# Gating products inside the layernorm ahead of the routing, and mixture weights built as a row on the chip: a two-block graph network with feed-forward stages

## The chip, the cores and the metric

One Trainium2 chip, one core. The time is that of the device for one execution of the whole kernel, in microseconds (us), as the median of three runs.

## What is computed

The reference takes a graph of 3125 nodes with 256 features and 103125 edges, and adds four residual stages to the node features, each on a layernorm of them. Two of the four matter here:

```python
# stage 2: experts; x is the layernorm of the node features
logits = einsum('bsd,de->bse', x, gate_w) + gate_b      # 16 experts
probs = softmax(logits)
top_probs, top_idx = top_k(probs, 2)
...
# stage 4: a mixture of depths over the nodes; x is again a layernorm
weights = (einsum('bsd,do->bso', x, wr) + br)[..., 0]    # one number a node
_, idx = top_k(weights, 1562); sel_idx = idx[:, :1561]
h = gelu(x[sel_idx] @ w1 + b1);  y = h @ w2 + b2         # hidden width 1024
y = y * weights[sel_idx]
processed = zeros_like(x).at[sel_idx].set(y);  out = processed + x
```

Stages 1 and 3 are graph attention networks with 8 heads and with three layers; the change leaves them alone.

## The kernel before

Everything is float32 in what follows. The nodes are 25 blocks of 128 (`NB`), the last with 53 rows. The program is a row of phases. A phase is a function under `@phase`: it allocates its semaphores, writes one instruction stream an engine, and at its end `run` clears its semaphores and puts a barrier of all engines. So nothing of a phase starts before everything of the phase ahead of it has ended, and a transfer that the phase's SyncE stream waits for holds up that end.

**From the first layernorm sum to the experts.** `node_phase` with the name n1 loads the input `x` and the attention output `y` in five parts of five blocks, adds them, takes the statistics, and normalizes block by block on VectorE (line 597). TensorE transposes each block's two halves (line 644) into one of four PSUM buffers, ScalarE copies them to `xt` (line 629). SyncE stores the sum to `x1` (two transfers, `store_nodes`) and the normalized rows to `xn1` (five transfers, line 544), and waits for all seven at the end (line 547). Then `router_phase` starts: it loads the gate's weights and bias, and TensorE multiplies each block of `xt` with the two halves of the gate's weights into one PSUM bank (lines 1466 to 1471):

```python
pe.wait_ge(s_in, 32)
for b in range(NB):
    for k in range(2):
        last = nc.tensor.matmul(ps[:, b * XE:(b + 1) * XE], xt[:, k, b * P:(b + 1) * P], gw[:, k, :],
                                start=k == 0, stop=k == 1)
last.then_inc(s_l, 1)
```

VectorE waits for the last of these (`s_l`), adds the bias (line 1508), and goes through softmax, top two, ranks and slots, a chain on VectorE with a few products between. `moe_phase` gathers rows of `xn1` by the slots.

**The mixture phase.** `node_phase` with the name n3 makes the last `xt` and `xn`, and `mod_phase` follows. Its SyncE stream loads wr, br, w1, b1, w2, b2 in this order, then the residual rows `res`. TensorE makes the weights as 50 products with one moving column (line 1842), one PSUM column a block, and then runs to the end without VectorE: hidden products of 320 columns for five blocks at a time (line 1855), and between them the output products of the five blocks before (line 1866). ScalarE applies the gelu (line 1886) and copies outputs to `ff` (line 1892). VectorE adds br to the weights (line 1906). SyncE stores them to `w_dram` (line 1814), waits, and loads them back broadcast to all partitions as a row of 3200 (line 1816). Against that row VectorE counts for each node how many weights are larger (lines 1913 to 1925), finds the nodes among the first 1561, and then, as `ff` comes, multiplies and adds into `res` (lines 1937, 1939), which SyncE stores in parts. GpSimd adds `xn` into `res` (line 1835) once `res` has landed.

What sets the order is each engine's own stream as written, and one in-order queue of transfers on SyncE. A float32 product is two weight loads and two matmul instructions in the trace, so 50 products are 100; a transpose is one of each. A name such as `xt1` or `n1_x` stands in the trace without its number.

## Time and profile before

| | |
|---|---|
| median of 3 runs | 4057.14 us (4055.54 to 4057.16) |
| the profiled execution's own time | 4054.18 us |
| its span | 4052.5 us |
| busy share of the span | PE 86%, PEld 64%, DVE 71%, ACT 59%, POOL 5% |
| mean granted TensorE clock | 0.947 |
| n1, from its first load's issue to the routing phase's first | 2042.92 to 2090.38 us |
| routing phase, to the experts' first load | 2090.38 to 2175.26 us |
| mixture phase, to the span's end | 3845.07 to 4052.5 us |

All times inside the trace count from the span's start. PE is TensorE's matmul, PEld its weight load, DVE VectorE, ACT ScalarE, POOL GpSimd, SP SyncE; a q behind a name is that engine's sequencer. A PEclk of 1.00 is the full clock, 2.4 GHz, and 0.50 the lower, 1.2 GHz. The duration of a merged row runs from the first instruction's start to the last one's end. Matmuls are pipelined: one lasts longer than the distance to the next.

### The profile page before, as it was taken

Reading aid. Unit: us, or ns where it says so; the run is one execution under the profiler, and the core shown is the slowest. Engines: PE = TensorE matmul, PEld = TensorE weight load, DVE = VectorE, ACT = ScalarE, POOL = GpSimd, SP = SyncE. Lnnn points to the kernel's source line nnn. Section 1 sums busy time; section 2 is a strip of 40 time slices with the busy share of each in tenths; the row PEclk is TensorE's granted clock in tenths of the full one; section 3 lists DMA queues with packets and bytes.
Section 4 is the critical chain, followed back from the end, with each engine's and each line's share of the span. In section 5 each row is a group of like instructions: output and inputs, shape, how many; then the busy total and the mean of one; then the engine's idle time right before and its main releaser. Section 6 shows DMA issues by size and latency. Waiting matters only on the chain. (4 is left out here: it accounts for less than half of the span.)

```text
span 4052.5 us, 69131 instructions
## 1 busy us (share of the span) xinstructions
PE 3497.2 (86%) x26175; PEld 2605.0 (64%) x26176; DVE 2880.4 (71%) x4370; ACT 2400.7 (59%) x3733; POOL 218.0 (5%) x212
## 2 busy tenths in 40 slices
PE   4989738888888888888835999689998999899799
PEld 2545436666666666666633566478887888788687
DVE  6989849999999999999934222365646654655456
ACT  3777628888888888888810111256665665444422
POOL 0000000000000000000001444100000000000010
PEclk9999969999999999999957999799999999999889
DMA  1222331111114111111145422233223232333220
GB/s 50 98 88 98 117 101 50 68 60 58 67 51 183 63 68 51 67 56 63 36 132 178 128 44 45 59 131 112 96 96 112 96 112 80 127 112 112 87 63 32
DMA packets 135864, 349.43 MB, mean 86 GB/s; under 512 B 28251, under 2 KB 106462, under 8 KB 117886
## 3 DMA queue, kind: packets, MB, share of 16 engines
q1 hardware_dynamic: 114840, 320.24, 22.3%
q0 software_dynamic: 13888, 20.07, 2.7%
q10 hardware_dynamic: 6822, 4.85, 0.4%
q8 instruction: 207, 3.39, 0.3%
q14 instruction: 107, 0.88, 0.1%
HBM read 279.91 MB, written 65.20 MB: 85 GB/s over the span
## 5 line engine op out<-in xcount | busy, mean ns | idle before, releaser
L919 PE MATMUL hd_psT<-ident,hd_scores 128*128 128x128 f32 (+1 forms) x5000 | 738.2, 286 | 31.8 <-ACT hd_scores L822 31.8
L831 ACT ACTIVATE hd_probsT<-hd_psT 128x768 f32<-128x768 f32 (+1 forms) x800 | 648.2, 835 | 187.3 <-PE hd_psT L919 186.4
L867 DVE SCALAR_TENSOR_TENSOR hd_scores<-hd_el,hx 128x3136 f32<-128x3136 f32 x200 | 695.5, 3478 | 24.4 <-DMA hd_mask<-mask_dram 18.4
L871 DVE CUSTOM_DVE_ANT_0 hd_scores<-hd_scores,hd_mask 128x3136 f32<-128x3136 f32 x200 | 684.0, 3420 | 8.6
L933 PE MATMUL hd_psO<-hd_probsT,hx 128*32 128x128 f32 (+1 forms) x10000 | 583.3, 286 | 101.0 <-ACT hd_probsT L831 100.2
L919 PEld LDWEIGHTS hd_psT<-ident,hd_scores 128*128 128x128 f32 (+1 forms) x5000 | 544.3, 143 | 185.5 <-issue 183.6
L822 ACT ACTIVATE hd_scores<-hd_scores,hd_negmax 128x1664 f32<-128x1664 f32 (+1 forms) x400 | 640.7, 1602 | 11.0 <-DVE hd_negmax L871 10.9
L1309 PE MATMUL ly_psO<-hx_a,ly_probsT 128*128 128x256 f32 x2500 | 583.1, 381 | 0.0
L1267 ACT ACTIVATE ly_probsT<-ly_psT 128x768 f32<-128x768 f32 (+1 forms) x300 | 249.3, 831 | 469.5 <-PE ly_psT L1298 469.4
L933 PEld LDWEIGHTS hd_psO<-hd_probsT,hx 128*32 128x32 f32 (+1 forms) x10000 | 322.8, 110 | 300.0 <-ACT hd_probsT L831 176.2
L1309 PEld LDWEIGHTS ly_psO<-hx_a,ly_probsT 128*128 128x128 f32 x2500 | 453.3, 189 | 71.2 <-issue 16.6
L366 PE MATMUL cnt<-onehot_c,onehot_dst_a 128*128 128x392 bf16 x1200 | 237.8, 335 | 89.9 <-DVE onehot_c L308 81.8
L308 DVE TENSOR_SCALAR onehot_c<-iotaC,stage_c 128x392 bf16<-128x392 f16 x1200 | 294.1, 314 | 0.0
L1309 PE MATMUL ly_psO<-hx_b,ly_probsT 128*128 128x256 f32 x1250 | 291.7, 381 | 0.0
L1298 PE MATMUL ly_psT<-ident,ly_scores 128*128 128x128 f32 x1875 | 258.9, 276 | 35.1 <-ACT ly_scores L1258 35.1
L366 PEld LDWEIGHTS cnt<-onehot_c,onehot_dst_a 128*128 128x128 bf16 x1200 | 135.1, 128 | 208.9 <-issue 113.0
L1258 ACT ACTIVATE ly_scores<-ly_scores,ly_negmax 128x1664 f32<-128x1664 f32 (+1 forms) x150 | 239.6, 1598 | 39.0 <-DVE ly_negmax L1179 38.5
L1298 PEld LDWEIGHTS ly_psT<-ident,ly_scores 128*128 128x128 f32 x1875 | 219.6, 141 | 62.7 <-ACT ly_scores L1258 35.8
L1179 DVE CUSTOM_DVE_ANT_0 ly_scores<-ly_scores,ly_mask 128x3136 f32<-128x3136 f32 x75 | 256.5, 3420 | 3.2
L1673 PE MATMUL moe_ps_h<-moe_w,moe_xT 128*128 x512 | 243.4, 598 | 8.6 <-SPq L1631 7.3
L1309 PEld LDWEIGHTS ly_psO<-hx_b,ly_probsT 128*128 128x128 f32 x1250 | 226.7, 189 | 35.5 <-issue 8.3
L1731 ACT ACTIVATE moe_hidden<-moe_ps_h 128x512 f32<-128x512 f32 x64 | 38.2, 597 | 326.6 <-PE moe_ps_h L1673 326.6
(298 smaller groups left out, 3805.2 us busy)
## 6 DMA issues: line engine op xcount, KB each, us to landing
ly_mask<-mask_dram SPq DMA_DIRECT2D x75, 1568.0 KB, 6.5
hd_mask<-mask_dram SPq DMA_DIRECT2D x50, 1568.0 KB, 6.8
mask_dram<-logc SPq DMA_DIRECT2D x200, 196.0 KB, 1.9
moe_w<-in_L_ffn_w SPq DMA_DIRECT2D x48, 512.0 KB, 10.9
hd_el<-el_dram SPq DMA_DIRECT2D x5, 1568.0 KB, 9.9
hd_el<-el_slope_dram SPq DMA_DIRECT2D x4, 1568.0 KB, 12.9
x<-n_x SPq DMA_DIRECT2D x2, 3072.0 KB
n_x<-in_x SPq DMA_DIRECT2D x8, 640.0 KB, 7.7
```

The lines of the kernel that those rows point to most:

```text
L308: last = nc.vector.tensor_scalar(oc[:, k, :], g["iotaC"][:, :], c[:, k:k + 1], None, ALU.is_equal)
L366: last = nc.tensor.matmul(o, ohA[:, s, :, k], ohC[:, s, k, :], start=k == 0 and not further, stop=True, skip_group_check=True)
L822: nc.scalar.activation(sc[:, u % 3, halves[j]], sc[:, u % 3, halves[j]], ACT.Exp, scale=-1.0, bias=nm[:, u % 3:u % 3 + 1], accum_out=den[: ...
L831: nc.scalar.activation(pT[:, gi % 2, 0:w], psT[gi % 2][:, 0:w], ACT.Copy).then_inc(s_ev, 1)
L867: nc.vector.scalar_tensor_tensor(sc[:, c, :], el[:, h, 0, :], hx[:, b, o:o + 1], el[:, h, 1, :], ALU.subtract, ALU.min).then_inc(s_lk, 1)
L871: nc.vector.tensor_tensor_reduce(out=sc[:, c, :], in0=sc[:, c, :], in1=mask[:, B % 2, :], scale=1.0, scalar=3.0e38, op0=ALU.add, op1=ALU.m ...
L919: last = nc.tensor.transpose(psT[gi % 2][0:r, t * P:(t + 1) * P], sc[:, u % 3, c0:c0 + r], g["ident"][:, :])
L933: last = nc.tensor.matmul(psO[B % 3][cg * CH:(cg + 1) * CH, h * P:(h + 1) * P], hx[0:r, tt, c0:c0 + CH], pT[0:r, gi % 2, t * P:(t + 1) * P ...
L1179: nc.vector.tensor_tensor_reduce(out=sc[:, c, :], in0=sc[:, c, :], in1=mask[:, B % 2, :], scale=1.0, scalar=3.0e38, op0=ALU.add, op1=ALU.m ...
L1267: nc.scalar.activation(pT[:, gi % 2, 0:w], psT[gi % 2][:, 0:w], ACT.Copy).then_inc(s_ev, 1)
L1298: last = nc.tensor.transpose(psT[gi % 2][0:r, t * P:(t + 1) * P], sc[:, B % 3, c0:c0 + r], g["ident"][:, :])
L1309: last = nc.tensor.matmul(psO[B % 2][:, 0:D], pT[0:r, gi % 2, t * P:(t + 1) * P], hx[B // NB % 2][0:r, tt, 0:D], start=tt == 0, stop=tt == ...
```

## The change

Two parts.

**Routing.** A new phase, `routed_nodes_phase`, holds n1 and the routing. It owns the tiles `x` and `xn`, the PSUM bank of the logits, and a semaphore `s_stored` that outlives n1. Inside n1 TensorE makes the gating products of block b-2 behind the transposes of block b, each waiting for ScalarE's copy of that block; the gate's weights are loaded behind n1's other loads. n1's SyncE no longer waits for its seven stores; the routing's SyncE does, at its end. The routing starts with the bias load alone, and VectorE waits for that in place of `s_l`. Since the new phase wraps two, one more clearing of semaphores and one more barrier stand behind the routing.

**Mixture weights.** TensorE makes the row itself: wr, one half at a time, broadcast to all 128 columns as the stationary operand, against `xt` as the moving one, in eight chunks of 400 columns over two PSUM banks (16 products, 32 matmul instructions). ScalarE adds br on its way to the row. VectorE gets each block's weights down the partitions by multiplying the block's piece of the row with the identity and summing. The store and the load of `w_dram` go. br is now awaited with wr, ahead of TensorE's first product.

```diff
 def node_phase(...):
+        if s_kept is not None:
+            s_out = s_kept
@@ sync
+                if gate is not None:
+                    sp.dma_start(gw[:, :, :], gate_dram.rearrange("(k p) n -> p k n", p=P)).then_inc(s_gw, 16)
...
-                if x_out is not None:
+                if x_out is not None and s_kept is None:
                     sp.wait_ge(s_out, 32 + (16 * NPART if xn_store is not None else 0))
@@ tensor
+            def gating(b):
+                pe.wait_ge(s_xt, b + 1)
+                for k in range(2):
+                    nc.tensor.matmul(logits[:, b * XE:(b + 1) * XE], xt[:, k, b * P:(b + 1) * P], gw[:, k, :],
+                                     start=k == 0, stop=k == 1)
+            if gate is not None:
+                pe.wait_ge(s_gw, 16)
             for b in range(NB):
...
                 last.then_inc(s_T, 1)
+                if gate is not None and b >= 2:
+                    gating(b - 2)
+            if gate is not None:
+                gating(NB - 2)
+                gating(NB - 1)
 def router_phase(...):
@@ sync
-            sp.dma_start(gw[:, :, :], a["L0_ffn_gate_w"].rearrange("(k p) n -> p k n", p=P)).then_inc(s_in, 16)
...
+            sp.wait_ge(s_kept, n_kept)
             sp.wait_ge(s_clear, 16 * len(spare))
@@ tensor
-            pe.wait_ge(s_in, 32)
-            for b in range(NB):
-                for k in range(2):
-                    last = nc.tensor.matmul(ps[:, b * XE:(b + 1) * XE], xt[:, k, b * P:(b + 1) * P], gw[:, k, :],
-                                            start=k == 0, stop=k == 1)
-            last.then_inc(s_l, 1)
@@ vector
-            dve.wait_ge(s_l, 1)
-            dve.wait_ge(s_in, 32)
+            dve.wait_ge(s_in, 16)
+@phase
+def routed_nodes_phase(nc, g, x_in, y_dram, x1, xn1, tok, wgt, tile_e, a):
+    with ExitStack() as ctx:
...
+        s_stored = new_semaphore(nc, g, "rn_s_stored")
...
+            node_phase(nc, g, "n1", xt, x_in=x_in, y=y, y_in=y_dram, x_out=x1, xn_out=xn, xn_store=xn1, x_tile=x,
+                       gate=(a["L0_ffn_gate_w"], gw, logits), s_kept=s_stored)
+        router_phase(nc, g, logits, s_stored, 32 + 16 * NPART, tok, wgt, tile_e, (x1, xn1), a)
 def mod_phase(...):
@@ sync
-            sp.dma_start(br[:, :], line(a["L1_ffn_br"], 1)).then_inc(s_in, 16)
+            sp.dma_start(br[:, :], line(a["L1_ffn_br"], 1)).then_inc(s_wr, 16)
...
-            sp.wait_ge(s_wt, 1)
-            sp.dma_start(g["w_dram"].rearrange("(b p) -> p b", p=P), wt[:, :], allow_slow_non_contiguous=True).then_inc(s_wd, 16)
-            sp.wait_ge(s_wd, 16)
-            sp.dma_start(row[:, :], line(g["w_dram"], NP)).then_inc(s_row, 16)
@@ tensor
-            pe.wait_ge(s_wr, 16)
-            for b in range(NB):
+            pe.wait_ge(s_wr, 32)
+            for c in range(WCHUNKS):
+                if c >= 2:
+                    pe.wait_ge(s_row, c - 1)
                 for k in range(2):
-                    last = nc.tensor.matmul(psw[:, b:b + 1], xt[:, k, b * P:(b + 1) * P], wr[:, k:k + 1],
-                                            start=k == 0, stop=k == 1)
-            last.then_inc(s_w, 1)
-            pe.wait_ge(s_in, 80)
+                    last = nc.tensor.matmul(psw[c % 2][:, 0:WCOLS], wr[:, k:k + 1].broadcast_to([P, P]),
+                                            xt[:, k, c * WCOLS:(c + 1) * WCOLS], start=k == 0, stop=k == 1)
+                last.then_inc(s_w, 1)
+            pe.wait_ge(s_in, 64)
@@ scalar
-            act.wait_ge(s_in, 80)
+            act.wait_ge(s_wr, 32)
+            for c in range(WCHUNKS):
+                act.wait_ge(s_w, c + 1)
+                nc.scalar.activation(row[:, c * WCOLS:(c + 1) * WCOLS], psw[c % 2][:, 0:WCOLS], ACT.Identity,
+                                     bias=br[:, :]).then_inc(s_row, 1)
+            act.wait_ge(s_in, 64)
@@ vector
-            dve.wait_ge(s_w, 1)
-            dve.wait_ge(s_in, 80)
-            nc.vector.tensor_scalar(wt[:, :], psw[:, 0:NB], br[:, :], None, ALU.add).then_inc(s_wt, 1)
             c.wait()
-            dve.wait_ge(s_wt, 1)
-            dve.wait_ge(s_row, 16)
+            for b in range(NB):
+                dve.wait_ge(s_row, ((b + 1) * P - 1) // WCOLS + 1)
+                nc.vector.scalar_tensor_tensor(spread[:, b, :], row[:, b * P:(b + 1) * P], 1.0, g["ident"][:, :],
+                                               ALU.mult, ALU.mult, accum_out=wt[:, b:b + 1]).then_inc(s_wt, 1)
+            dve.wait_ge(s_wt, NB)
+            dve.wait_ge(s_row, WCHUNKS)
             dve.wait_ge(s_k, 5)
+            dve.wait_ge(s_in, 64)
```

How the instructions stand on TensorE at the first place, n1 to the routing, before (a product counts once here; `n_ps` holds transposes, `rt_ps` the logits):

```order
L634 UNCONDITIONAL_BRANCH
L644 MATMUL n_ps<-ident,n_xn 128x128 x50
L492 UNCONDITIONAL_BRANCH
L1464 UNCONDITIONAL_BRANCH
L1469 MATMUL rt_ps<-rt_gate_w,xt 128x16 x50
L1476 MATMUL rt_ps_within<-rt_one_hot,rt_before 128x384
```

And with the change, the beginning and the end of that stretch (`rn_ps_logits` is the logits' bank):

```order
L641 UNCONDITIONAL_BRANCH
L658 MATMUL n_ps<-ident,rn_xn 128x128 x6
L646 MATMUL rn_ps_logits<-gate_w,xt 128x16 x2
L658 MATMUL n_ps<-ident,rn_xn 128x128 x2
...
L658 MATMUL n_ps<-ident,rn_xn 128x128 x2
L646 MATMUL rn_ps_logits<-gate_w,xt 128x16 x6
L492 UNCONDITIONAL_BRANCH
L1481 UNCONDITIONAL_BRANCH
L1487 MATMUL rt_ps_within<-rt_one_hot,rt_before 128x384
```

Six transposes stand ahead of the first products, then two and two take turns, and the last three blocks' products end the phase; the routing has none left.

On ScalarE at the second place, n3 to the mixture phase, with the change (line 636 copies n3's transposes, 1908 makes the row, 1919 is the gelu):

```order
L636 ACTIVATE xt<-n_ps 128x2x128 x25
L492 UNCONDITIONAL_BRANCH
L1903 UNCONDITIONAL_BRANCH
L1908 ACTIVATE mod_weights_row<-mod_psw,mod_br 128x400 x8
L1919 ACT_TABLE_LOAD
L1919 ACTIVATE mod_hidden<-mod_h,mod_b 128x320 x32
```

The eight passes of the row stand where there was nothing before; the table load ahead of the gelu stays where it was, and none is added.

## Rows read from the trace of the kernel before

**Rows 1.** the chain that ended last, in time order: start us, us, what
```profile
3845.07 2.02 DMA mod_wr<-in_L_ffn_wr
...
3847.14 21.49 PE mod_w L1842 x100
3868.63 37.52 PE mod_h L1855 x128
```

**Rows 2.** timeline, layernorm to routing: start us, us, engine, what [idle before <-releaser]
```profile
2072.91 8.19 PE L644 MATMUL n_ps<-ident,n_xn 128*128 128x128 f32 x50 [37.59 <-DVE n_xn L597]
2073.64 7.88 ACT L629 ACTIVATE xt<-n_ps 128x256 f32<-128x256 f32 x25 [1.57 <-PE n_ps L644]
2074.18 8.95 SPq L544 DMA_DIRECT2D xn_dram<-n_xn  x5
2090.38 0.38 SPq L1434 DMA_DIRECT2D rt_gate_w<-in_L_ffn_gate_w  x1
...
2094.08 21.52 PE L1469 MATMUL rt_ps<-rt_gate_w,xt 128*128 128x16 f32 x100 [12.97 <-DMA rt_gate_b<-in_L_ffn_gate_b]
...
2115.63 0.57 DVE L1508 TENSOR_TENSOR rt_logits<-rt_ps,rt_gate_b 128x400 f32<-128x400 f32 x1 [24.72 <-PE rt_ps L1469]
```

**Rows 3.** DMA issue of that stretch: count, KB, us from issue to landing
```profile
rt_gate_b<-in_L_ffn_gate_b SPq DMA_DIRECT2D x1, 8.0 KB, 3.2
```

**Rows 4.** stretches: us, busy PE, PEld, DVE, ACT, POOL, PEclk, DMA, GB/s
```profile
2074.90:2075.90 1.00, 1.00 (x7) 1.00 (x7) 1.00 (x4) 0.90 (x3) 0.00 (x0) 0.62 1.04 348
...
2094.00:2115.00 21.00, 20.92 (x98) 20.92 (x99) 0.00 (x0) 0.00 (x0) 0.21 (x1) 0.50 0.11 9
```

**Rows 5.** timeline of TensorE's weight loads in the second network's projection
```profile
2627.46 0.40 PEld L1114 LDWEIGHTS np_e<-ident,hx_a 128*128 128x128 f32 x2
2627.78 0.25 PEld L1099 LDWEIGHTS np_x<-ident,np_xn 128*128 128x128 f32 x2
2628.00 0.74 PEld L1107 LDWEIGHTS np_h<-wx,np_xT 128*128 128x128 f32 x4
2628.77 0.41 PEld L1114 LDWEIGHTS np_e<-ident,hx_a 128*128 128x128 f32 x2
```

**Rows 6.** the gating products' instructions: ns min/median/max
```profile
L1469 PEld LDWEIGHTS rt_ps<-rt_gate_w,xt x100: 288/333/337, 2094.1 to 2115.2; 128*128 128x128 f32 x100
L1469 PE MATMUL rt_ps<-rt_gate_w,xt x100: 374/374/396, 2094.1 to 2115.2; 128*128 128x16 f32 x100
```

**Rows 7.** timeline, last layernorm to the mixture phase
```profile
3835.53 8.75 ACT L629 ACTIVATE xt<-n_ps 128x256 f32<-128x256 f32 x25 [1.57 <-PE n_ps L644]
...
3845.49 0.46 SPq L1806 DMA_DIRECT2D mod_br<-in_L_ffn_br  x1
...
3867.80 13.70 POOL L1835 TENSOR_TENSOR mod_res<-mod_res,xn 128x6400 f32<-128x6400 f32 x1 [21.72 <-DMA mod_res<-x]
...
3868.49 28.78 PE L1855 MATMUL mod_h<-xt,mod_w 128*128 128x320 f32 x95
...
3872.35 0.53 ACT L1886 ACTIVATE mod_hidden<-mod_h,mod_b 128x320 f32<-128x320 f32 x1
...
3891.20 3.34 DVE L1918 TENSOR_SCALAR_CACHE_REDUCE mod_junk<-mod_weights_row,mod_weights 128x2997 bf16<-128x2997 f32 x1 [22.29 <-DMA mod_weights_row<-w_dram]
...
3894.46 0.35 DVE L1921 SCALAR_TENSOR_TENSOR mod_junk<-mod_weights_row,mod_weights,mod_low 128x128 bf16<-128x128 f32 x1
```

**Rows 8.** stretches of that phase, columns as in rows 4
```profile
3847.00:3852.00 5.00, 4.86 (x23) 4.86 (x24) 0.00 (x0) 0.00 (x0) 0.00 (x0) 0.52 0.91 268
3852.00:3857.00 5.00, 5.00 (x25) 5.00 (x25) 0.00 (x0) 0.00 (x0) 0.00 (x0) 0.50 0.95 301
3873.00:3875.00 2.00, 2.00 (x6) 1.29 (x5) 0.00 (x0) 0.56 (x2) 2.00 (x1) 0.63 0.04 0
```

**Rows 9.** timeline: its last hidden block, and VectorE behind the counting
```profile
3992.24 17.39 PE L1855 MATMUL mod_h<-xt,mod_w 128*128 128x320 f32 x64
...
4013.54 0.42 DVE L1937 TENSOR_TENSOR mod_tmp<-hx_b,mod_b 128x256 f32<-128x256 f32 x1 [4.40 <-ACT hx_b L1892]
```

More of the change, by code:

```diff
@@ L485, in node_phase @@
 def node_phase(nc, g, name, xt, x_in=None, y=None, y_in=None, x_out=None, unit=False, xn_out=None, xn_store=None,
-               gelu=False, layernorm=True, add_loops=False):
+               gelu=False, layernorm=True, add_loops=False, x_tile=None, gate=None, s_kept=None):
     with ExitStack() as ctx:
@@ L500, in node_phase @@
         if layernorm:
-            x = sb("x", [P, NB, D])
+            x = x_tile if x_tile is not None else sb("x", [P, NB, D])
             xn = xn_out if xn_out is not None else sb("xn", [P, NB, D])
@@ L512, in node_phase @@
             loop = lambda i: lv[:, i, :].rearrange("p (q o) -> p q o", o=1)
+        if gate is not None:
+            gate_dram, gw, logits = gate
+            s_gw = sem("s_gate_w")
+        if s_kept is not None:
+            s_out = s_kept
         block = ctx.enter_context(nc.Block())
@@ L646, in _ @@
                 last.then_inc(s_T, 1)
+                if gate is not None and b >= 2:
+                    gating(b - 2)
+            if gate is not None:
+                gating(NB - 2)
+                gating(NB - 1)
 @phase
@@ L1421, in router_phase @@
         s_din, s_dout = sem("s_diagonal_in"), sem("s_diagonal_out")
[L1422 removed]
         psw = ctx.enter_context(nc.psum_tensor("rt_ps_within", [P, 512], F32))
         pst = ctx.enter_context(nc.psum_tensor("rt_ps_total", [P, 512], F32))
[L1425 to L1426 removed]
+        s_in, s_io, s_c, s_z, s_e, s_one, s_hot, s_rank, s_zero, s_clear, s_sel, s_inv = (
+            sem(n) for n in ("s_in", "s_io", "s_c", "s_z", "s_e", "s_one", "s_hot", "s_rank", "s_zero", "s_clear",
                              "s_selectors", "s_inverse"))
@@ L1577, in _ @@
             step(nc.vector.tensor_copy(wgt[:, :], back[:, 2, :]))
+@phase
+def routed_nodes_phase(nc, g, x_in, y_dram, x1, xn1, tok, wgt, tile_e, a):
+    with ExitStack() as ctx:
+        tile = lambda n, s: ctx.enter_context(nc.sbuf_tensor(f"rn_{n}", s, F32))
+        s_stored = new_semaphore(nc, g, "rn_s_stored")
+        x = tile("x", [P, NB, D])
+        xn = tile("xn", [P, NB, D])
+        logits = ctx.enter_context(nc.psum_tensor("rn_ps_logits", [P, 512], F32))
+        with ExitStack() as first:
+            xt = first.enter_context(nc.sbuf_tensor("xt1", [P, 2, NP], F32))
+            y = first.enter_context(nc.sbuf_tensor("y1", [P, NB, D], F32))
+            gw = first.enter_context(nc.sbuf_tensor("gate_w", [P, 2, XE], F32))
+            node_phase(nc, g, "n1", xt, x_in=x_in, y=y, y_in=y_dram, x_out=x1, xn_out=xn, xn_store=xn1, x_tile=x,
+                       gate=(a["L0_ffn_gate_w"], gw, logits), s_kept=s_stored)
+        router_phase(nc, g, logits, s_stored, 32 + 16 * NPART, tok, wgt, tile_e, (x1, xn1), a)
 @phase
@@ L1790, in mod_phase @@
         hid = sb("hidden", [P, 2, MB, CT * P])
+        spread = sb("spread", [P, NB, P])
+        WCHUNKS = 8
+        WCOLS = NP // WCHUNKS
         res = sb("res", [P, NB, D])
@@ L1794, in mod_phase @@
         pso = [ctx.enter_context(nc.psum_tensor(f"mod_o{i}", [P, 512], F32)) for i in range(2)]
-        psw = ctx.enter_context(nc.psum_tensor("mod_w", [P, 512], F32))
-        names = ("s_wr", "s_in", "s_k", "s_w", "s_wt", "s_wd", "s_row", "s_res", "s_sum", "s_h", "s_hid", "s_o", "s_ff", "s_c",
+        psw = [ctx.enter_context(nc.psum_tensor(f"mod_psw{i}", [P, 512], F32)) for i in range(2)]
+        names = ("s_wr", "s_in", "s_k", "s_w", "s_wt", "s_row", "s_res", "s_sum", "s_h", "s_hid", "s_o", "s_ff", "s_c",
                  "s_y1", "s_y2", "s_st")
-        (s_wr, s_in, s_k, s_w, s_wt, s_wd, s_row, s_res, s_sum, s_h, s_hid, s_o, s_ff, s_c, s_y1, s_y2, s_st) = (
+        (s_wr, s_in, s_k, s_w, s_wt, s_row, s_res, s_sum, s_h, s_hid, s_o, s_ff, s_c, s_y1, s_y2, s_st) = (
             sem(n) for n in names)
@@ L1979, in program @@
         tile_e = sb("tile_expert", [1, NT], I32)
-        with ExitStack() as s:
-            xt = s.enter_context(nc.sbuf_tensor("xt1", [P, 2, NP], F32))
-            with nc.sbuf_tensor("y1", [P, NB, D], F32) as y:
-                node_phase(nc, g, "n1", xt, x_in=a["x"], y=y, y_in=y_dram, x_out=x1, xn_store=xn1)
-            router_phase(nc, g, xt, tok, wgt, tile_e, (x1, xn1), a)
+        routed_nodes_phase(nc, g, a["x"], y_dram, x1, xn1, tok, wgt, tile_e, a)
         moe_phase(nc, g, tile_e, tok, wgt, xn1, x1, a)
```

7 lines of the change are left out of this document (1 added, 6 removed).

## The prediction, made before the change was run

> **What bounds the kernel now.** I read the chain that ended last first. It is followed back to the start of the mixture phase and is TensorE nearly throughout: 2.02 us for the load of wr, 21.49 us for the mixture weights, then hidden and output products to the end [rows 1]. So in that phase a microsecond saved on TensorE ahead of the hidden products is one off the total, and the work on VectorE is not: late in the phase VectorE sits idle 4.40 us until ScalarE hands it an output [rows 9].
>
> Then I read the timeline from the second layernorm to the routing, which says what ends each wait there. TensorE's transposes end at 2072.91 + 8.19 = 2081.1, ScalarE's copies at 2081.5, and SyncE has issued its last store by 2083.1, but the next phase begins at 2090.38 [rows 2]. The end of n1 thus hangs on the stores. Then TensorE idles 12.97 us in all until the gate's bias has landed, runs 21.52 us, and VectorE starts at 2115.63, released by TensorE [rows 2]. Behind that the routing is a chain on VectorE, so what counts there is the start of line 1508.
>
> Last I read the granted clock in both places. It is 0.50 in the whole stretch of gating products [rows 4], and rises only some way into the hidden products: its mean over 3873 to 3875 is 0.63 [rows 8], so the last 0.5 us of those ran at full clock and it rose at 3874.5, 6.0 us after the hidden products began at 3868.49 [rows 7].
>
> The profiled execution took 4054.18 us, 3.0 less than the median of 4057.14. The sum is made against the former, and 3.0 is added at the end. A measurement of this kernel can tell some 0.2% (8 us) from no change.
>
> **Part one, n1 and the routing.** Removed from the path: the stores' wait, and the gate's weight load ahead of the products. Added to n1's TensorE stream: 100 instructions to 50. At 1.2 GHz one gating instruction comes every 21.52 / 100 = 0.215 us [rows 2]. Each lasts 0.374 us and its load 0.333 [rows 6], so loads overlap products, and with 16 columns moving it is the 128x128 load that sets 0.215. A transpose has a load of the same shape, so I give it 0.215 too. The lower bound is the pace VectorE gave it, 8.19 / 50 = 0.164. With 150 x 0.215 = 32.3 us from 2072.91 the stream ends at 2105.2 (lower bound 2102.6), the last product 0.16 later.
>
> The change of phase then costs what it costs between n3 and the mixture phase, where no store holds it: ScalarE ends at 3835.53 + 8.75 = 3844.28 [rows 7] and the first load goes out at 3845.07 [rows 1], 0.8 us. So the routing begins at 2106.2, and now waits for the bias alone, which takes 3.2 us from its issue [rows 3]. VectorE starts at 2109.4 in place of 2115.6: **6.2 us gained**. The stores were down by 2090 before, so they hide under the longer products and the wait at the routing's end, 60 us on, costs nothing. The weight load behind n1's loads has over 10 us until the first transpose.
>
> What goes the other way is the clearing and barrier behind the routing. No row shows one alone. It costs between nothing and a whole change of phase, 0.8; I take half, **0.4 us lost**.
>
> The clock is my main choice here. In n1 it rose within a stretch of pure transposes: its mean over 2074.9 to 2075.9 is 0.62 [rows 4], so it rose near 2075.7, 2.8 us after they began [rows 2]. For all 21 us of pure gating products it stayed at 0.50 [rows 4]. In the change six transposes come alone, 1.3 us of them, and then four gating instructions to two transposes. I take the mixture for the kind that holds two thirds of it: 1.2 GHz throughout. The Trainium skill, page "TensorE: Matmul & The Clock Gate", section "Part 4: PE-mode transpose", says that transposes don't count as activity that brings the full clock. By that rule the forecast for this part is certain and its rival below impossible. The trace does not agree: only transposes ran when the clock rose in n1 [rows 2, 4].
>
> **Part two, the mixture phase.** TensorE now waits for br as well, issued at 3845.49 [rows 7]. Its landing isn't shown; the gate's bias, broadcast in the same way, took 3.2 us [rows 3], wr's load 2.02 [rows 1]. I take 3.2: TensorE starts at 3848.7, not 3847.14 (1.6 lost; with 2.0 it would be 0.4).
>
> Its 32 instructions have 400 columns. At full clock 64 of 320 columns took 17.39 us, 0.272 each [rows 9], so 400 take 0.340, and twice that at half clock. They are dense from the start, and in the rows at hand such work waits 2.8 to 6.0 us for the clock; I take the middle, 4.4, of which half is lost: 32 x 0.340 + 2.2 = 13.1 us, to 3861.8. With 2.8 and 6.0 it is 0.8 less or more.
>
> Are w1, b1, w2, b2 there by then? They are 2.2 MB, and at 268 and 301 GB/s [rows 8] 1.34 MB had moved by 3852 and the rest by 3855. Yes. So hidden products begin at 3861.8 in place of 3868.49, and at full clock: before, the first 6.0 us at half clock held 11 instructions (6.0 / 0.544), now they take 3.0. The eleventh ends at 3864.8 in place of 3874.5: **9.7 us gained**, and from there TensorE does what it did.
>
> ScalarE's eight passes: one over 320 columns took 0.53 [rows 7], so 400 cost 0.53 to 0.66, against 1.36 us that TensorE needs for a chunk at full clock; two banks cover it. VectorE's 25 products with the identity: one of that size took 0.35 [rows 7], with the read of the sum I take 0.4 each. They follow the chunks; the last four come behind the last chunk, and counting starts near 3864.5 in place of 3891.20 [rows 7]. These 27 us are worth nothing: the 22.29 us wait for the row [rows 7] was never TensorE's. They are also the cover if GpSimd's add of 13.70 us [rows 7], so far beside an idle VectorE, and the counting now slow each other. If that cover went, the end of VectorE's 25 residual blocks would be late next.
>
> **Sum.** 6.2 - 0.4 + 9.7 = 15.5. 4054.2 - 15.5 = 4038.7, and with 3.0 for the median **4041.7 us**. The likeliest case's own range: the pace of transposes (2.6 less), the barrier and br's load (0.4, 1.2), the clock's rise (0.8), and up to 1.6 either way because later phases meet the clock at another moment: 4038 to 4045.
>
> **Rivals.**
> *The clock rises in n1's mixture.* For it: transposes alone raised it [rows 4]. Against it: they are a third of the instructions, and their neighbours left it at 0.50 for 21 us. In the second network's projection, at full clock, eight loads take 1.31 us, four of them under 258 columns [rows 5], which at 0.272 x 258/320 = 0.219 [rows 9] leaves 0.108 for each load-bound one. 13 instructions at 0.215, then 137 at 0.108 make 17.6 us in place of 32.3: 14.7 more gained, **4027 us**.
>
> *Hidden products don't start earlier*, because their weights share the queues with the residual rows' load, which lands at 3867.80 [rows 7]. Then only 0.7 us of part two is left: 4054.2 - 6.2 + 0.4 - 0.7 + 3.0 = **4050.7**. Against it speaks the sum of bytes above.
>
> *Slower: the turns on TensorE in n1.* Each change between transposes and products has a semaphore wait in front. If the load behind it can't go ahead under the instruction before, load and product stand one after the other, 0.333 + 0.374 [rows 6] in place of 0.215: 0.49 us, 50 changes, 24.6 us. 4041.7 + 24.6 = **4066**. It outweighs the gains from 32 such changes on. Against it: in the projection, three kinds take turns with waits between them, and the eight loads show no such gap [rows 5].
>
> That the stores are still waited for in n1 is no rival of weight: by 2105 they are long down.
>
> **Chances.** The forecast 0.80, the clock in the mixture 0.07, hidden products held 0.08, exposed loads 0.03, and 0.02 for gains too small to measure. Faster by over 0.2% are the first two, 0.87; within 0.2% the third and the last, 0.10; slower 0.03. The range 4036 to 4051 holds the likeliest case with its bounds and reaches the second rival; it leaves out the ends at 4027 and 4066.
>
> **What would show it.** In n1: 150 instructions on TensorE in some 32 us at 0.50, the next phase within 1 us of their end, line 1518 (the old 1508) 36.5 us after the first transpose, 42.7 before. In the mixture phase: the first 400-column product 3.6 us after the phase's start, a pace that halves some 4 us on, hidden products at 0.272 from the first on and 16.7 us after the phase's start, 23.4 before. It is wrong if the clock in n1 reads 1.00 behind the first blocks, if the first hidden product waits for a DMA, or if VectorE's residual blocks end the phase without idle time before them.

## The result and the profile after

Medians of six runs each: 4055.41 us before (4053.95 to 4057.16), **4038.91 us after** (4037.66 to 4040.6). The ratio is 0.9958 with a 95% interval of 0.9946 to 0.9969: faster by 0.42%. The profiled execution took 4037.66 us (4054.18 before), its span is 4036.0, the mean granted clock 0.949. Three other executions (one of the kernel before, beside the runs below, one of part two alone, one of the last run) took 1.3 to 2.3 times as long at a granted clock of 0.63 or less, and the medians leave them out.

The chain that ended last in the kernel after, in time order (start us, us, what), to be laid beside [rows 1]:

```profile
3838.28 3.38 DMA mod_br<-in_L_ffn_br
...
3841.70 13.51 PE mod_psw L1870 x32
3855.22 34.45 PE mod_h L1883 x128
```

It starts with br's load now, 3.38 us, in place of wr's. The phase begins at 3837.86, TensorE 3.84 us later, and the hidden products 17.4 us after the phase (23.6 before). The phase lasts 4036.0 - 3837.86 = 198.1 us, where it lasted 4052.5 - 3845.07 = 207.4: **9.3 us** from part two.

Timeline of the kernel after, n1 to the routing (columns as in rows 2), beside [rows 2]:

```profile
2073.09 1.51 PE L658 MATMUL n_ps<-ident,rn_xn 128*128 128x128 f32 x6 [37.88 <-DVE rn_xn L604]
...
2075.10 0.67 PE L658 MATMUL n_ps<-ident,rn_xn 128*128 128x128 f32 x2
...
2076.28 0.67 PE L658 MATMUL n_ps<-ident,rn_xn 128*128 128x128 f32 x2
...
2100.20 2.58 PE L646 MATMUL rn_ps_logits<-gate_w,xt 128*128 128x16 f32 x12
...
2103.58 0.34 SPq L1451 DMA_DIRECT2D rt_gate_b<-in_L_ffn_gate_b  x1
...
2106.10 0.57 DVE L1518 TENSOR_TENSOR rt_logits<-rn_ps_logits,rt_gate_b 128x400 f32<-128x400 f32 x1 [1.98 <-DMA rt_gate_b<-in_L_ffn_gate_b]
```

TensorE's 150 instructions run from 2073.09 to 2102.78, 29.7 us, and a round of two transposes and four products takes 2076.28 - 2075.10 = 1.18 us. The routing begins 0.8 us behind the last product, and VectorE waits 1.98 us for the bias. From the first transpose to its logits are 33.0 us, before 42.7 [rows 2]: 9.7 us. The windows of that stretch (columns as in rows 4) have the clock at 0.50 all along; the last of them:

```profile
2090.00:2100.00 10.00, 10.00 (x53) 10.00 (x53) 0.00 (x0) 3.35 (x9) 0.00 (x0) 0.50 0.00 0
```

At the routing's end, timeline before and then after (VectorE's first and last instruction behind the inverse, then the experts' first load):

```profile
2173.12 0.36 DVE L1574 COPY rt_slot_source<-rt_ps_inverse 128x192 f32<-128x192 f32 x1 [8.37 <-PE rt_ps_inverse L1485]
...
2174.06 0.19 DVE L1577 COPY slot_gate<-rt_slot_source 128x64 f32<-128x64 f32 x1
2175.26 0.93 SPq L1624 DMA_DIRECT2D moe_w<-in_L_ffn_w  x2
```

```profile
2164.73 0.36 DVE L1584 COPY rt_slot_source<-rt_ps_inverse 128x192 f32<-128x192 f32 x1 [9.51 <-PE rt_ps_inverse L1496]
...
2165.67 0.19 DVE L1587 COPY slot_gate<-rt_slot_source 128x64 f32<-128x64 f32 x1
2167.26 0.42 SPq L1651 DMA_DIRECT2D moe_w<-in_L_ffn_w  x1
```

Before, VectorE's last instruction ends at 2174.25 and the load goes out 1.01 us later; now it is 1.40: the additional clearing and barrier cost 0.39 us. The routing's chain itself is 59.8 us long, from 2106.10 to 2165.86, where it was 58.6; VectorE waits 9.51 us for TensorE's inverse in place of 8.37. That is 1.1 us lost that the prediction didn't have, and it is the clock: from the logits' addition to the first of the 100 products of the inverse are 38.7 us in both traces, but the granted clock rose 3.3 us into them before and 5.6 us into them now, and they took 18.7 and 19.8 us. Over all traces on record it rises 2.9 to 6.0 us in, and they take 18.5 to 20.0; the run with GpSimd's add moved, whose routing is the change's, has 2.9 and waits only 8.20 us. So this loss is no added work. But four of the five traces with the change's routing have 5.6 to 6.0 us, and whether the change tends to meet the clock so is open. From the first transpose to the experts' load part one leaves 9.7 - 1.1 - 0.4 = **8.2 us**. The experts start 8.0 us earlier, the mixture phase 7.2: 0.8 are given back on the way, and 7.2 + 9.3 = 16.5 is the whole difference.

Timeline of the kernel after in the mixture phase, beside [rows 7]:

```profile
3837.86 0.37 SPq L1835 DMA_DIRECT2D mod_wr<-in_L_ffn_wr  x1
...
3841.70 13.51 PE L1870 MATMUL mod_psw<-xt,mod_wr 128*128 128x400 f32 x32 [5.18 <-DMA mod_br<-in_L_ffn_br]
...
3856.85 3.34 DVE L1953 TENSOR_SCALAR_CACHE_REDUCE mod_junk<-mod_weights_row,mod_weights 128x2997 bf16<-128x2997 f32 x1
...
3859.19 13.72 POOL L1861 TENSOR_TENSOR mod_res<-mod_res,xn 128x6400 f32<-128x6400 f32 x1 [20.31 <-DMA mod_res<-x]
...
3860.11 12.94 DVE L1956 SCALAR_TENSOR_TENSOR mod_junk<-mod_weights_row,mod_weights,mod_low 128x128 bf16<-128x128 f32 x1
```

TensorE runs its 32 wide products in 13.5 us. ScalarE's pass over a chunk takes 0.59 us. VectorE counts from 3856.85 in place of 3891.20. And one of its instructions, of a line whose usual 0.35 us are in [rows 7], takes 12.94 us, nearly for the 13.72 us of GpSimd's add. Windows (columns as in rows 4) for the clock under the wide products:

```profile
3846.00:3847.00 1.00, 1.00 (x4) 0.52 (x3) 0.28 (x4) 0.00 (x0) 0.00 (x0) 0.61 1.10 347
3847.00:3848.00 1.00, 1.00 (x5) 0.56 (x3) 0.18 (x1) 0.59 (x1) 0.00 (x0) 1.00 1.06 328
```

It rose at 3846.8 (1.00 for 0.22 of that window), 5.1 us into the products, and the hidden products all ran at full clock.

### The profile page after: what moved, and what is told of

Read it like the earlier page. It is cut to its first block and busy times, and to the rows that moved or that the text cites. A ratio compares the mean times of both kernels' runs of the same rounds, so it can differ in the third digit from the quotient of the medians.

```text
span 4036.0 us, 69063 instructions
## 1 busy us (share of the span) xinstructions
PE 3489.8 (86%) x26107; PEld 2593.9 (64%) x26108; DVE 2899.2 (72%) x4419; ACT 2408.4 (60%) x3741; POOL 218.2 (5%) x212
```

## Experiments

The questions: does each part pay by itself what the traces say; which half of part one pays; what do the remaining waits cost; does the clock in n1 hang on the gating products being narrow; what held the one VectorE instruction. Each run stands beside runs of the kernel before on the same chip, and differences below are those of the medians.

**Part one alone.** The changed n1 and routing with the mixture phase of before.

> Part one alone: the changed n1 and routing, and the mixture phase of before. Theory A (the two parts pay separately, each where the traces show it): the experts' first load comes 8.0 us earlier, as in the change (2167.26 against 2175.26), the mixture phase's hidden products again start 23.4 us after the phase's start, and the total is 7 to 9 us below the kernel before, near 4047.5. Theory B (the 0.8 us that the change gives back between the experts and the mixture phase belongs to the shift itself and comes back here in another size): the experts' first load is early by the same 8.0 us, but the total moves by less than 6 or by more than 10 us, and the difference lies in the second network or the experts.

Measured: 4049.47 us against 4057.67, 8.2 less; ratio 0.9979 (0.9970 to 0.9988). The stretch from the first transpose to the experts' load is 94.3 us (before 102.35), the mixture phase 207.6 us. Theory A.

**Part two alone.** The n1 and routing of before with the changed mixture phase.

> Part two alone: the n1 and routing of before, and the changed mixture phase. Theory A: the mixture phase lasts 198.1 us in place of 207.4, hidden products begin 17.2 to 17.4 us after its start, and the total is 9.3 us below the kernel before, near 4046.1 (8.5 to 10). The sum of this gain and that of part one alone is the change's 16.5 within 1.5 us. Theory B (the mixture phase profits from something that part one moved, say the phase's place in the clock's rise): the phase is then longer than 200 us here.

Measured: 4048.74 us, 8.9 less; ratio 0.9978 (0.9969 to 0.9987). The mixture phase lasts 198.2 us, the first stretch 102.4. Theory A, and 8.2 + 8.9 = 17.1 against the change's 16.5: the parts add up. Beside them the second network's attention layers took 2.7 us more in this profile than in that of before, with the same instructions (from the first mask load to n3, 1156.4 us before, 1156.6 in the change, 1159.1 here); that moves a single total, and its cause stays open.

**Only the stores' wait moved.**

```diff
-            node_phase(..., gate=(a["L0_ffn_gate_w"], gw, logits), s_kept=s_stored)
+            node_phase(..., s_kept=s_stored)
@@ router, sync
+            sp.dma_start(gw[:, :, :], ...).then_inc(s_in, 16)
@@ router, tensor
+            pe.wait_ge(s_in, 32)
+            for b in range(NB):
...
```

> The gating products go back to the start of the routing, with the load of the gate's weights; the stores are still awaited only at the routing's end. The mixture phase is the changed one. Theory A (the stores' wait was worth its full length): n1 ends with ScalarE's copies, the routing begins near 2082.3 in place of 2090.4 before, its two loads take as long as they did, VectorE starts line 1518 8.1 us earlier than before and 1.6 us later than in the change: total near 4040.5. Theory B (the loads stand behind the stores in the same queue or share its engines): TensorE's first gating product comes only when the stores are down, near 2090.5 to 2091 in place of 2094.1 before, VectorE starts near 2112 to 2112.5, and the total is near 4045. In that case the gating inside n1 is worth some 6 us by itself, in theory A hardly 2.

Measured: 4046.00 us, 11.7 less; ratio 0.9969 (0.9957 to 0.9980). 8.9 of them are part two's, so part one gives 2.8 in this form; in its trace the first transpose to the experts' load takes 99.1 us in place of 102.35, 3.3 less. Its timeline (columns as in rows 2):

```profile
2073.91 8.19 PE L658 MATMUL n_ps<-ident,rn_xn 128*128 128x128 f32 x50 [37.52 <-DVE rn_xn L604]
...
2075.17 8.90 SPq L551 DMA_DIRECT2D xn_dram<-rn_xn  x5
2084.99 0.75 SPq L1452 DMA_DIRECT2D gate_w<-in_L_ffn_gate_w  x1
...
2090.88 21.51 PE L1488 MATMUL rn_ps_logits<-gate_w,xt 128*128 128x16 f32 x100 [8.78 <-DMA rt_gate_b<-in_L_ffn_gate_b]
...
2112.43 0.57 DVE L1527 TENSOR_TENSOR rt_logits<-rn_ps_logits,rt_gate_b 128x400 f32<-128x400 f32 x1 [26.90 <-PE rn_ps_logits L1488]
```

Two things hold it. The phase can't end before SyncE has issued its last store, at 2075.17 + 8.90 = 2084.07, and only then do the gate's loads go out (2084.99), behind stores that are still moving, so that the bias lands 5.0 us after its issue and not 3.2 [rows 3]. The first product comes 17.0 us after the first transpose, in place of 21.2 before. Theory B: moving the wait is worth 3 us, and 5 come from gating inside n1, which also puts the rest of the stores under products.

**Only the gating moved.**

```diff
-                if x_out is not None and s_kept is None:
+                if x_out is not None:
                     sp.wait_ge(s_out, 32 + (16 * NPART if xn_store is not None else 0))
@@ router, sync
-            sp.wait_ge(s_kept, n_kept)
```

> The gating products stay inside n1; the stores are awaited at n1's end again. Otherwise the change. Theory A (TensorE's stream ends at 2102.8, 12 us after the stores are down, so that wait ends nothing): no difference from the change, 4038.9 within 0.5 us, and the routing's first load again 0.8 us after TensorE's last product. Theory B (the wait at the routing's end costs something there, or the one at n1's end does): a difference from the change of 0.5 us or more, at the end of n1 or of the routing.

Measured: 4039.44 us, 18.2 less; ratio 0.9956 (0.9943 to 0.9969), which the change's own 0.9958 can't be told from. The routing's first load goes out at 2102.22, 0.8 us behind the last product (2101.42), as in the change. Theory A: with the gating in n1, keeping the stores' wait for later is worth nothing that can be told. Its trace has the experts' load 1.72 us behind VectorE's last instruction, in place of 1.40; I can't say why.

**Three small waits less.**

```diff
-@phase
 def routed_nodes_phase(...):
-        s_stored = new_semaphore(nc, g, "rn_s_stored")
+        s_stored = nc.alloc_semaphore("rn_s_stored")
@@ n1, sync
+                    sp.dma_start(gb[:, :], ...).then_inc(s_gw, 16)
@@ mixture, tensor and scalar
-            pe.wait_ge(s_wr, 32)
+            pe.wait_ge(s_wr, 16)
-            act.wait_ge(s_wr, 32)
+            act.wait_ge(s_br, 16)
```

> The change with three small edits, each readable in its own place: the gate's bias is loaded inside n1, so the routing starts without a load; the outer phase clears and waits for nothing of its own (the kept semaphore is cleared with the routing's); TensorE waits for wr alone in the mixture phase, ScalarE for br. Theory A (each wait is on the path that sets the end): VectorE starts the logits' addition within 0.5 us of the routing phase's start, in place of 2.5; the experts' first load comes 1.0 us behind VectorE's last instruction, in place of 1.4; the first 400-column product starts 2.1 us after its phase's start, in place of 3.8. Together 2.0 + 0.4 + 1.7 = 4.1 us below the change, near 4034.8. Theory B (the earlier start of the wide products is given back, since the clock rises at the same place in the phase and ScalarE can't empty the two banks until br has landed at 3.4): the hidden products start less than 0.9 us earlier in their phase, and the total is 3.3 us or less below the change.

Measured: 4035.99 us, 21.3 less; ratio 0.9947 (0.9933 to 0.9961). Its medians put it 2.9 to 4.8 us below the change, depending on which runs of before they are held against; its span is 5.1 us shorter. In their places: VectorE adds the bias 0.45 us after the routing's start; the experts' load follows VectorE's last instruction by 1.00 us; the wide products start 2.07 us into their phase. The chain that ended last, and the clock (columns as in rows 4):

```profile
3835.38 2.02 DMA mod_wr<-in_L_ffn_wr
...
3837.45 12.69 PE mod_psw L1870 x32
3850.14 34.45 PE mod_h L1883 x128
```

```profile
3837.00:3838.00 1.00, 0.55 (x1) 0.50 (x2) 0.00 (x0) 0.00 (x0) 0.00 (x0) 0.73 0.31 17
...
3840.00:3841.00 1.00, 1.00 (x3) 0.43 (x2) 0.00 (x0) 0.41 (x1) 0.00 (x0) 0.57 1.01 406
3841.00:3842.00 1.00, 1.00 (x5) 0.56 (x4) 0.70 (x6) 0.18 (x1) 0.00 (x0) 1.00 1.22 200
```

The mixture phase lasts 195.5 us, 2.6 less than in the change, not 1.7. The clock, at 1.00 since n3's transposes, fell at 3837.45, just as the products began (1.00 for 0.45 of the first window), and is back at 1.00 at 3840.9, 3.4 us in, where the change needed 5.1. Theory A in the places; theory B, that the clock would rise at the same place in the phase and take the gain back, is refuted: it rose 5.5 us into the phase, in the change 8.9. All four traces with this wait have 3.4 to 3.7 us and 12.7 us for the products; the six with the wait for br as well have 5.0 to 5.5 us and 13.5 to 13.7.

**Gating products ahead of the norm.** On top of the three edits: since (x - mean) · g = x · (g - mean of g), TensorE can multiply the sums themselves, and the reciprocal deviation is a factor behind it.

```diff
@@ n1, vector, behind the second part's sum
+                            nc.vector.tensor_tensor(gw[:, k, :], gw[:, k, :], gmean[:, 0:XE], ALU.subtract)
@@ n1, tensor
-                    pe.wait_ge(s_n, b + 1)
+                    pe.wait_ge(s_sum, b // PART + 1)
-                    transpose(ps[b % 4][...], xn[:, b, ...], ident)
+                    transpose(ps[b % 4][...], x[:, b, ...], ident)
@@ routing, vector
+            step(nc.vector.tensor_tensor(lg, blocks(ps), wide(rs[:, 1, :]), ALU.mult))
```

> The three edits of the kernel with three small waits less, and one more: n1's transposes and gating products take the sum x itself instead of its normalized rows, from the first part's sum on, with gate weights whose mean over the features has been taken away; the routing multiplies the logits with the reciprocal deviation of each node before it adds the bias (one VectorE instruction of 0.57 us more). Theory A (TensorE's 150 instructions, 29.7 us, were the end of n1 and stood behind the normalization for no reason): TensorE starts near 2051 and ends near 2081, VectorE's normalization ends near 2081 as before, SyncE has issued its last store near 2084, and the routing starts near 2085 in place of 2103.6. That is 18 us below the kernel with three small waits less, near 4017. Theory B (ScalarE's copies and VectorE's sums in n1 delay each other, or the normalization is held up because its square root stands among ScalarE's copies): the routing starts after 2090 and the gain is below 14 us.

Measured: **4017.12 us**, 40.2 less than before; ratio 0.9901 (0.9885 to 0.9916), and 18.9 below the kernel with three small waits less. Theory A. Its timeline shows what is left:

```profile
2056.75 1.04 PE L664 MATMUL rn_ps_logits<-gate_w,xt 128*128 128x16 f32 x4 [3.54 <-DVE gate_w L597]
...
2073.18 0.18 DVE L602 TENSOR_SCALAR rn_rs<-n_mv 128x25 f32<-128x25 f32 x1
...
2075.16 1.28 ACT L643 ACT_TABLE_LOAD   x1
...
2076.46 0.23 ACT L643 ACTIVATE rn_rs<-rn_rs 128x25 f32<-128x25 f32 x1
...
2078.80 6.82 SPq L559 DMA_DIRECT2D xn_dram<-rn_xn  x5
...
2082.73 2.58 PE L664 MATMUL rn_ps_logits<-gate_w,xt 128*128 128x16 f32 x12
```

TensorE stood 3.54 us for the centred weights. VectorE's variance is there at 2073.36, but its reciprocal starts at 2076.72: the root stands in ScalarE's stream behind the copy of block 17, which ended at 2075.15, and then ScalarE loaded the square root's table for 1.28 us. TensorE's last product ends at 2085.3, SyncE's last store is issued at 2085.6.

**Gating products of 128 columns.** The change, with 112 columns of zeros beside the 16 of the gate.

```diff
-            gw = first.enter_context(nc.sbuf_tensor("gate_w", [P, 2, XE], F32))
+            gw = first.enter_context(nc.sbuf_tensor("gate_w", [P, 2, P], F32))
-                    nc.tensor.matmul(logits[:, b * XE:(b + 1) * XE], xt[...], gw[:, k, :], ...)
+                    nc.tensor.matmul(logits[:, b * XE:b * XE + P], xt[...], gw[:, k, :], ...)
```

> The change with gating products of 128 moving columns in place of 16 (the other 112 are zeros, written over the logits' columns of later blocks before those are made). It is the test of the rival in which the clock rises in n1. Theory A (the mixture's products leave the clock at 0.50 whatever their width, since transposes rise by themselves and these stand between): TensorE's stream in n1 lasts 29.7 to 33 us at 0.50, the total is 4039 to 4042. Theory B (with 128 columns moving the mixture is of the kind of the pure transposes, which also move 128 and rose after 2.8 us): the granted clock reads 1.00 from some 3 to 6 us into the stream, the stream lasts 17.5 to 20 us, VectorE's logits start 10 to 12 us earlier, total near 4028.

Measured: 4030.57 us, 26.7 less; ratio 0.9932 (0.9918 to 0.9947), 8.3 us below the change by the medians and 10.2 by what each is below its runs of before. Windows and timeline:

```profile
2075.00:2080.00 5.00, 5.00 (x24) 4.98 (x25) 5.00 (x17) 1.93 (x5) 0.00 (x0) 0.50 1.04 345
2080.00:2085.00 5.00, 5.00 (x43) 5.00 (x42) 2.60 (x9) 2.62 (x7) 0.00 (x0) 0.91 1.02 331
2085.00:2090.00 5.00, 5.00 (x47) 5.00 (x46) 0.00 (x0) 2.77 (x8) 0.00 (x0) 1.00 0.89 294
```

```profile
2074.99 1.51 PE L665 MATMUL n_ps<-ident,rn_xn 128*128 128x128 f32 x6 [37.91 <-DVE rn_xn L610]
...
2093.14 1.50 PE L652 MATMUL rn_ps_logits<-gate_w,xt 128*128 128x128 f32 x12
...
2097.94 0.57 DVE L1525 TENSOR_TENSOR rt_logits<-rn_ps_logits,rt_gate_b 128x400 f32<-128x400 f32 x1 [1.97 <-DMA rt_gate_b<-in_L_ffn_gate_b]
```

The clock rose at 2080.9 (1.00 for 0.82 of that window), 5.9 us into the stream, and stayed there. The 150 instructions take 19.7 us in place of 29.7, and VectorE's logits come 23.0 us after the first transpose in place of 33.0. Theory B: with eight times the columns the same number of instructions takes 10 us less. In none of the eight traces with 16 columns in this mixture did the clock leave 0.50. Until the rise the padding costs a little: a round takes 1.28 us at 0.50, where it took 1.18 with 16 columns.

**GpSimd's add behind the counting.**

```diff
@@ gpsimd
+            pool.wait_ge(s_cd, 1)
             pool.wait_ge(s_res, 32)
@@ vector, behind the counting
+            dve.sem_inc(s_cd, 1)
```

> The change with GpSimd's add of the residual rows held back until VectorE has counted. In the change one VectorE instruction of line 1956 (two operands in SBUF, 128 columns, otherwise 0.35 us) lasted 12.94 us, just while the 13.72 us add ran. Theory A (the add keeps such an instruction out for its whole length): all 25 of line 1956 take 0.27 to 0.35 us, the counting ends 12.6 us earlier, and the add, now beside an idle VectorE, takes 13.7 us as before. The total doesn't move, 4038.9 within 1 us, as VectorE idles 9.6 us late in the phase in the change and here about 8.5. Theory B (something else held it, such as the residual rows' load or ScalarE's first gelus): one instruction of that time still lasts long.

Measured: 4039.74 us in a single run, which gives no interval. All 25 of the line and the add, then the first and a late residual block of VectorE:

```profile
L1958 DVE SCALAR_TENSOR_TENSOR mod_junk<-mod_weights_row,mod_weights,mod_low x25: 271/347/350, 3862.1 to 3962.4; 128x128 bf16<-128x128 f32 x24, 128x53 bf16<-128x53 f32 x1
```

```profile
3964.02 13.72 POOL L1863 TENSOR_TENSOR mod_res<-mod_res,xn 128x6400 f32<-128x6400 f32 x1 [123.08 <-DVEq L1969]
...
3977.77 0.42 DVE L1975 TENSOR_TENSOR mod_tmp<-hx_b,mod_b 128x256 f32<-128x256 f32 x1 [13.89 <-POOL mod_res L1863]
...
3999.09 0.43 DVE L1975 TENSOR_TENSOR mod_tmp<-hx_b,mod_b 128x256 f32<-128x256 f32 x1 [8.39 <-ACT hx_b L1927]
```

No instruction of the line takes more than 0.35 us. The add takes its 13.72 us beside an idle VectorE, which waits 13.89 us for it and later still idles 8.39. Theory A: the add held it, and it cost the total nothing.

**Root and mean early; last stores in the routing.** The gating ahead of the norm, mended where its trace showed waits: the mean is subtracted behind the first sum, and ScalarE takes a root at the start of the phase. In a second kernel the routing also issues the last two stores.

```diff
-                    if gate is not None and p == 1:
+                    if gate is not None and p == 0:
+                    nc.scalar.activation(table, avg[:, 0:1], ACT.Sqrt)
@@ second kernel only: n1's sync, then the routing's
-                    for p in range(NPART):
+                    for p in range(NPART - 2):
+            for p in range(NPART - 2, NPART):
+                sp.dma_start(xn1[...], xn[...]).then_inc(s_kept, 16)
```

> The kernel with gating before the norm, mended at the two places where its trace shows a wait: the gate weights' mean is subtracted behind the first part's sum, not the second's (TensorE stood 3.5 us for it), and ScalarE takes a square root of a constant at the phase's start, so that its table is there when the deviations' turn comes (it loaded one for 1.28 us on the path, 3.4 us in all from VectorE's variance to its reciprocal). Theory A: TensorE's stream ends near 2082 in place of 2085.3 and VectorE's normalization near 2082.5 in place of 2085.2; SyncE's last store, which hangs on both the rows and the queue, is then what ends n1, near 2084; the routing starts 43.0 - 1.5 to 2 = 41 to 41.5 us after n1's first load is issued, total 4015 to 4016. Theory B (the stores' issue is limited by the queue alone, 6.4 MB at some 340 GB/s from 2069 on): SyncE's last issue stays near 2085.6 and the total is the same as before, 4017.

> The kernel with root and mean early, and the last two of the five stores of normalized rows issued at the start of the routing, ahead of its zero rows. Theory A (the issue of the stores is the last thing that holds n1): the routing starts within 1 us of the later of TensorE's last product and VectorE's last row, some 40 us after n1's first load is issued, 1 to 2 us earlier than in the kernel it is made from; the stores and the zero rows behind them are down long before the routing's end; total near 4014. Theory B: no difference of 0.5 us or more from the kernel it is made from, or a loss, since the transfers of the routing now wait behind 1.3 MB of stores and one of them is awaited at its end.

Measured: 4015.47 us for the first, 43.7 less than before, ratio 0.9896 (0.9879 to 0.9912); 4013.90 us for the second, 45.3 less, ratio 0.9891 (0.9871 to 0.9911). Timelines of the first and of the second:

```profile
2072.71 0.22 ACT L644 ACTIVATE rn_rs<-rn_rs 128x25 f32<-128x25 f32 x1 [1.03 <-DVE rn_rs L603]
...
2075.05 8.81 SPq L560 DMA_DIRECT2D xn_dram<-rn_xn  x5
...
2079.26 2.58 PE L668 MATMUL rn_ps_logits<-gate_w,xt 128*128 128x16 f32 x12
```

```profile
2084.03 1.58 SPq L1481 DMA_DIRECT2D xn_dram<-rn_xn  x2
```

In the first the root comes 0.03 us behind the variance, TensorE ends at 2081.8, SyncE's last issue at 2083.9, and the routing begins 41.3 us after n1's first load, 42.9 before: theory A. In the second it begins 40.1 us after it, 0.8 behind TensorE's last product; but from there to the experts' load are 61.3 us in place of 60.5, and of the 1.2 us 0.45 are left. What takes the rest is the clock in the inverse: it rose 4.7 us into those products in place of 3.1, and VectorE waited 9.07 us for them in place of 8.29. The totals of the two can't be told apart.

## Why the prediction was right, and where its sizes were off

The sign, the size (15.5 us forecast, 16.5 measured in the profiled executions) and the places were right. The forecast of 4041.7 is 2.8 us above the median; 1.0 of that is the gain, and 1.8 the step from the profiled execution to the median, for which I added 3.0, and which is 1.2 in the runs beside the change (4055.41 - 4054.18). That 15.5 came so near to 16.5 is in part luck, since errors of both signs met: the way from the first transpose to VectorE's logits gave 3.5 more than forecast; the first transpose came 0.2 later, the inverse took 1.1 longer, 0.8 were lost behind the experts, and part two gave 0.4 less.

| step | forecast | measured |
|---|---|---|
| TensorE's 150 instructions in n1 | 32.3 us at 0.50 | 29.7 us at 0.50 |
| change of phase behind them | 0.8 | 0.8 |
| the bias, from the phase's start | 3.2 | 2.5 |
| first transpose to VectorE's logits (42.7 before) | 36.5 | 33.0 |
| the routing's chain behind that | as before | 1.1 longer |
| additional clearing and barrier | 0.4 | 0.4 |
| TensorE's start in the mixture phase | 3.6 | 3.8 |
| wide products | 13.1 | 13.5 |
| hidden products' start in the phase | 16.7 | 17.4 |
| part two | 9.7 | 9.3 |

**The pace in n1** is the term that was mis-sized, 32.3 us for 29.7, but not through the transposes. I gave each kind of instruction 0.215 us, and in a stretch of its own kind each does take that at 0.50: the last twelve products 2.58 us, the last one's own time included, and ten transposes of before 2.40. The 0.164 that I named as the lower bound is a mean over two clocks, because the clock rose 2.8 us into those 50 transposes [rows 2, 4]. Where it rose 6.0 us into them, in the run of part two alone, the same 50 took 9.11 us. Timelines of before, then of that run:

```profile
2072.91 2.40 PE L644 MATMUL n_ps<-ident,n_xn 128*128 128x128 f32 x10 [37.59 <-DVE n_xn L597]
```

```profile
2073.96 9.11 PE L644 MATMUL n_ps<-ident,n_xn 128*128 128x128 f32 x50 [37.61 <-DVE n_xn L597]
```

What the sum lacked is the turn from transposes to products. Timeline of the kernel after in two narrow windows (a row holds only what runs in its window):

```profile
2076.52 0.42 PE L658 MATMUL n_ps<-ident,rn_xn 128*128 128x128 f32 x1
2076.74 0.23 PE L646 MATMUL rn_ps_logits<-gate_w,xt 128*128 128x16 f32 x1
...
2076.81 0.59 PE L646 MATMUL rn_ps_logits<-gate_w,xt 128*128 128x16 f32 x2
```

The second transpose starts at 2076.52, the first product 0.22 us later, but the second product only 0.07 us behind the first; from there it is 0.21 again. That short step makes the round 1.18 us in place of six times 0.215, or 1.29. With 128 columns moving the round took 1.28: the short step is gone. Why a narrow product is passed so quickly there, no run shows. And that the stream ended on my lower bound is luck: the bound stood for faster transposes, and they weren't faster.

**The bias** took 2.5 us as the routing's first load; the 3.2 of [rows 3] was that of a load behind another one. In the mixture phase, where two loads follow each other, 3.2 was right (3.38).

**The clock in n1** was my main choice, and it stayed at 0.50 as forecast. But the reason was put too loosely: I gave the mixture to "the kind that holds two thirds of it". The 128-column run keeps the kinds, their counts and their order, changes only the products' width, and there the clock rose. The Trainium skill's rule that transposes don't count as activity (page "TensorE: Matmul & The Clock Gate", section "Part 4: PE-mode transpose") can't be tested by this run, since wide products stand between its transposes. The trace of before is against it, where only transposes ran when the clock rose 2.8 us after they began [rows 2, 4], and so are the two runs that kept that n1: 6.0 us in part two alone, 3.0 where only the stores' wait moved.

**The clock in the mixture phase** rose after 5.1 us, inside the 2.8 to 6.0 of the rows and 0.7 later than the middle I took, half of which is lost; TensorE started 0.2 us later than forecast. Together they are the hidden products' 0.7. Part two is then (23.6 - 17.4) + (37.5 - 34.5) = 9.3: the later start, and the first hidden block at full clock [rows 1]. The runs with TensorE waiting for wr alone show the other outcome, 12.7 us in place of 13.5.

**The rivals.** Hidden products were not held by loads: they follow the wide products without a gap. Exposed weight loads at the turns would have made a round of 1.29 us longer by about 1; it took 1.18. VectorE's residual blocks did not end the phase: it still idled 9.63 us for ScalarE's output at 3997.06. The clock's rise is a true possibility of the hardware, at another width than this kernel has.

**What I hadn't seen** is that the moved wait and the moved products pay for the same microseconds: the wait alone gives some 3 us of part one, the products alone all of its 8.2, both together no more. The sum was right because it took n1's end from TensorE's stream.

## What to carry to other kernels

When work moves onto an engine's stream in front of a phase's end, the new end is the longest of the streams, and two edits that shorten different ones don't add: give each its own time before crediting both. Then ask what the moved work needs: the gating products needed the sums, not the norm, and starting them there was worth 17 to 19 us (17.1 in the traces up to the experts' load, 18.9 by the medians) where moving them had been worth 8. And where a stretch of narrow fp32 products stands at half clock, try once what the granted clock does with zeros beside their columns: while the weight load sets the pace they cost little.

## What the runs showed of the hardware

**An add on GpSimd kept a VectorE instruction out for 12.94 us.** The instruction has two operands in SBUF and takes 0.35 us otherwise; it started 0.9 us after the add and finished at 3873.05, 0.14 us behind it. The long pass before it, with one such operand, took its usual time, 1.0 of its 3.34 us beside the add. The Trainium skill, page "SBUF — State Buffer", section "Who interferes with whom", has it as a rule: such an instruction and a GpSimd instruction that reads SBUF exclude each other for the whole length of the first to start. The runs agree: with the add moved, all 25 took 0.35 us or less. The prediction had asked only whether the two would slow each other.

**With 128 moved columns in place of 16 the granted clock read 1.00 from 5.9 us on**, in the same mixture with transposes that stayed at 0.50 in all eight traces with 16: 29.7 us became 19.7.

**The same products took another time from one execution to the next**, with the moment at which the clock rose: the 100 products of the routing's inverse 18.5 us where it rose 2.9 us behind their start, 20.0 where it rose 6.0 us behind it. So a single profile can differ by more than 1 us in a stretch whose instructions are the same.

**Stores delay the next phase twice**: in the run that moved only their wait, SyncE had issued the last one only 10.2 us after TensorE's first transpose, and a load issued behind them took 5.0 us to land, against 3.2 and 2.5 elsewhere.
